# A graph layer with scatter-add: GpSimd's scatters run 16 pipeline steps behind the edges in place of 4

## The reference, cut to what matters

```python
h = max(layernorm(x), 0)
S = h[src]                                   # one row for each edge
def edge_nn(x, W, b):                        # the same weights twice
    t = relu(x @ W.T + b)
    return relu(t @ W.T + b)
msgs = edge_nn(S, W_rel[rel], b_rel[rel])
agg = segment_sum(msgs, dst, n_nodes)        # scatter-add over destinations
gates = agg @ W_ih.T + b_ih + b_hh           # i, f, g, o; f is not used
c = sigmoid(i) * tanh(g)
hn = sigmoid(o) * tanh(c)
y = relu(relu(hn @ W1.T + b1) @ W2.T + b2) @ W3.T + b3
out = x + y
```

## Time and profile before

| | us |
|---|---|
| median of 3 runs | 2260.63 (2260.33 to 2261.53) |
| the profiled execution's own time | 2269.79 |
| its span, first to last instruction | 2268.1 |
| TensorE busy | 2080.7 |
| VectorE busy | 1755.9 |
| ScalarE busy | 1627.2 |
| GpSimd busy | 1187.8 |

### The profile page before, as it was taken

One profiled execution on the slowest core, in us unless ns is written; L12 is line 12 of the kernel. 1 busy time (PEld: TensorE's weight loads), 2 busy tenths in 40 slices (PEclk: granted clock), 3 DMA queues, 4 the chain that ended last, 5 costly groups with the idle time before them and its releaser, 6 DMA issues.

```text
span 2268.1 us, 51837 instructions
## 1 busy us (share of the span) xinstructions
PE 2080.7 (92%) x14224; PEld 1405.7 (62%) x14225; DVE 1755.9 (77%) x4311; ACT 1627.2 (72%) x3364; POOL 1187.8 (52%) x917
## 2 busy tenths in 40 slices
PE   5858767767999999999999999999999999999996
PEld 4746555555666666666666666666666666445553
DVE  8537555555888888888888888888888887788886
ACT  2437655555888888888888888888888887666663
POOL 0036777777766665666666666666666644100000
PEclk7559999898999999999999999999999999999998
DMA  9954555557789898889888988888888988988886
GB/s 383 425 207 93 95 95 100 98 97 141 135 174 185 170 180 174 179 170 175 175 178 173 178 177 180 178 178 183 170 178 175 180 153 162 193 188 191 190 188 156
DMA packets 400606, 396.90 MB, mean 175 GB/s; under 512 B 263738, under 2 KB 343158, under 8 KB 394360
## 3 DMA queue, kind: packets, MB, share of 16 engines
q0 software_dynamic: 91200, 157.34, 40.8%
q1 hardware_dynamic: 306788, 238.12, 40.0%
q10 hardware_dynamic: 2516, 0.14, 0.1%
HBM read 185.88 MB, written 156.97 MB: 151 GB/s over the span
## 4 chain that ended last, share of the span: by engine, by line
PE 78%; issue 7%; POOL 5%; ACT 3%; DMA 3%; DVE 3%; another core or an unknown queue 1%; POOLq 0%; DVEq 0%; ACTq 0%; SPq 0%
PE bank L1469 33%; PE bank L1435 9%; PE bank L1416 9%; PE bank L1483 6%; PE bank L1508 5%; PE bank L1452 4%; PE bank L1398 3%; PE bank L1492 3%; POOL agg L664 2%; POOL xg L648 2%; DMA agg<-summed,scatter_idx 2%; PE bank L1308 2%; PE bank L1409 2%; PE bank L1427 1%; DMA a_lo<-row_lo 1%
## 5 line engine op out<-in xcount | busy, mean ns | idle before, releaser
L664 POOL DMA_INDIRECT agg<-summed,scatter_idx x400 | 665.5, 1664 | 501.4 <-ACT summed L724 261.4
L1469 PE MATMUL bank<-a_hi,ihT 128*128 128x512 f16 x2400 | 714.0, 379 | 2.4 <-DMA a_lo<-row_lo 2.2
L648 POOL DMA_INDIRECT xg<-in_x,src_ring x400 | 426.1, 1065 | 271.0 <-DMA src_ring<-src_slot 138.1
L1469 PE MATMUL bank<-a_lo,ihT 128*128 128x512 f16 x1200 | 454.8, 379 | 0.0
L1469 PEld LDWEIGHTS bank<-a_hi,ihT 128*128 128x128 f16 x2400 | 234.4, 98 | 213.0 <-issue 2.3
L1435 PE MATMUL bank<-relT,h_hi 128*128 x1600 | 321.5, 275 | 0.0
L1416 PE MATMUL bank<-s_hi,relT 128*128 128x256 f16 x1600 | 292.9, 278 | 0.0
L672 POOL DMA_DIRECT2D y<-in_x x100 | 133.4, 1334 | 298.0 <-DVE y L1202 287.6
L1077 DVE SCALAR_TENSOR_TENSOR h_lo<-bank,h_hi 128x512 f16<-128x512 f32 x200 | 137.5, 688 | 120.4 <-ACT h_hi L751 114.6
L757 ACT ACTIVATE xn<-xg,shift,rstd 128x256 f32<-128x256 f32 x400 | 216.4, 591 | 10.3 <-DVE shift L1111 10.3
L1070 DVE SCALAR_TENSOR_TENSOR s_lo<-bank,s_hi 128x512 f16<-128x512 f32 x200 | 136.4, 682 | 111.2 <-ACT s_hi L730 73.4
(11 more groups left out here) (197 smaller groups left out, 4642.4 us busy)
## 6 DMA issues: line engine op xcount, KB each, us to landing
agg_in<-agg SPq DMA_DIRECT2D x100, 512.0 KB
y<-in_x POOLq DMA_DIRECT2D x100, 512.0 KB
out<-y SPq DMA_DIRECT2D x100, 512.0 KB
agg<-zeros SPq DMA_DIRECT2D x24, 2112.0 KB, 15.8
dst_ring<-dst_rows SPq DMA_DIRECT2D x200, 128.0 KB
xg<-in_x,src_ring POOLq DMA_INDIRECT x400
agg<-summed,scatter_idx POOLq DMA_INDIRECT x400
src_ring<-src_slot SPq DMA_DIRECT2D x200, 1.0 KB
```

The costliest lines, as they stand in the source:

```text
L648: nc.gpsimd.indirect_dma_start(out=xg[:, k.slot(8), t, :], out_offset=None, in_=x[:, :], in_offset=bass.IndirectOffsetOnAxis(ap=src_ring[: ...
L664: nc.gpsimd.indirect_dma_start(out=agg[:, :], out_offset=bass.IndirectOffsetOnAxis(ap=scatter_idx[:, k.slot(8), t:t + 1], axis=0), in_=sum ...
L1469: last = nc.tensor.matmul(N_C[c % 2][:, 0:UNIT], lhs, rhs, start=i == 0, stop=i == len(todo) - 1)
```

## The change

The scatter of pair k moves from GpSimd's step k+4 to k+16. `summed` gets 16 slots in place of 4, `scatter_idx` 16 in place of 8. ACT's copy of the sums of pair at-4 now waits for the scatter of pair at-20, which GpSimd issues at its step at-4, as before. DVE's row numbers of pair at-3 now wait for the scatter of pair at-19, which is issued at step at-3 (before: at-7). Because a unit needs its quarter's scatters, NB goes from 54 to 66, N0 from 60 to 72 and LAST from 270 to 282. Slots must divide the unroll, so the loop bodies have 16 steps.

```diff
+SUM_SLOTS = 16
+SCATTER_LAG = 16
-NB = QUARTER_PAIRS + 4
+NB = QUARTER_PAIRS + SCATTER_LAG
 N0 = NB + 6
...
-        scatter_idx = sb("scatter_idx", [P, 8, 2], I32)
-        summed = sb("summed", [P, 4, 2, D])
+        scatter_idx = sb("scatter_idx", [P, SUM_SLOTS, 2], I32)
+        summed = sb("summed", [P, SUM_SLOTS, 2, D])
...
-        RUN = dict(loops=((16, 40), (72, 184), (216, 248)), unroll=8)
+        RUN = dict(loops=((80, 176), (224, 256)), unroll=16)
...
-                k = at - 4
+                k = at - SCATTER_LAG
...
-                            out_offset=bass.IndirectOffsetOnAxis(ap=scatter_idx[:, k.slot(8), t:t + 1], axis=0),
-                            in_=summed[:, k.slot(4), t, :], in_offset=None, compute_op=ALU.add).then_inc(scattered, 16)
+                            out_offset=bass.IndirectOffsetOnAxis(ap=scatter_idx[:, k.slot(SUM_SLOTS), t:t + 1], axis=0),
+                            in_=summed[:, k.slot(SUM_SLOTS), t, :], in_offset=None, compute_op=ALU.add).then_inc(scattered, 16)
...
-                    wait_from(act, scattered, (k.n - 3) * 32)
-                    nc.scalar.copy(summed[:, k.slot(4), :, :].rearrange("p t d -> p (t d)"),
+                    wait_from(act, scattered, (k.n - SUM_SLOTS + 1) * 32)
+                    nc.scalar.copy(summed[:, k.slot(SUM_SLOTS), :, :].rearrange("p t d -> p (t d)"),
...
-                    wait_from(dve, scattered, (k.n - 7) * 32)
-                    nc.vector.tensor_tensor(scatter_idx[:, k.slot(8), :], idx_f[:, k.slot(4), :], spare_row[:, :],
+                    wait_from(dve, scattered, (k.n - SUM_SLOTS + 1) * 32)
+                    nc.vector.tensor_tensor(scatter_idx[:, k.slot(SUM_SLOTS), :], idx_f[:, k.slot(4), :], spare_row[:, :],
                                             ALU.min).then_inc(idx_ready, 1)
```

## The result

| kernel | median us | lowest to highest | profiled execution, span |
|---|---|---|---|
| before | 2261.08 | 2260.33 to 2265.3 (4 runs) | 2269.79, 2268.1 |
| after | 2307.21 | 2300.84 to 2314.52 (4 runs) | 2300.84, 2298.8 |

The ratio is 1.0201, 95% interval 1.0168 to 1.0235: slower by 46 us, where the forecast had 17.5, and beyond the range's upper end of 2290.

The account below looks back on a forecast made before the run. PE was taken to bound the mixed and units-alone stages, the scatter cycle the later edge steps. +11.2 (edge steps) + 6.3 (DMA load at the end) = +17.5 us took the median from 2260.6 to 2278.1; range 2267 to 2290.

Parts of the forecast that it names:

- The cycle itself: Later edge steps paced by scatters: the 6.81 us scatter cycle stays, larger rings free nothing; 0, bounds 0 and 27 us.
- Twelve more edge steps: Edge-only stage: scatters start 12 early steps of 5.08 us later, less 12 x 4.15 us of PE work; +11.2 us.
- Loops: Jumps back of the 16-step bodies: nothing to gain or lose, 0; bounds 0 and 6 x 1.4 us.
- rival 3: Loop ends: jumps back to 16-step bodies stall, 6 x 2.5, some 15 us, total 2293; chance 7%.
- The stage with both: Edges and units together: scatters no longer wait for sums, PE is at 100%; 0.
- The end, DMA load: Units alone: the last 12 scatters load the DMA engines and slow transposes, 4.5 x 1.39 = 6.3 us; bounds 0 and 10.
- The end, chain: Units alone: GpSimd falls 15.6 us back at cycles of 6.93, some 20 us slack covers it; 0, upper bound 26.
- 2: Units alone: with scatter cycles of 8 us or more SP waits for scatters, +11.2 + 6.3 + 8, 2286; chance 12%.
- Rival 4: Edge stage: scatter chain freed from sums runs at GpSimd's own 6.40 us, 20 us back, 2258 or 2251; chance 9%.
- 5: Edge stage: no change in total, early edge steps at 4.15 to 4.5 us or half the chain gain, 2262; chance 6%.
- four signs: Would be wrong: scatter cadence below 6.6, early steps below 4.8, PE gaps at loop-body ends, SP waiting for scatters at L593.

Follow-up runs that it names:

- lag16_small_x: After in straight code without loops, x adds of GpSimd's steps 203 to 215 moving 16 of 128 rows: 2283.81 us, ratio 1.0119 to before.
- lag16_straight_2: After with no hardware loop, every step straight code, on one of the usual chips: 2288.78 us, ratio 1.0144 to before.
- lag16_free12: After in straight code, last 12 pairs scattered each into its own tensor, no wait between them, SP waiting for 188 pairs: 2278.5 us, ratio 1.0093 to before.
- lag16_straight_skip12: After in straight code, the last 12 pairs not scattered, SP waiting for 188 pairs: 2271.96 us, ratio 1.0065 to before.
- lag4_ring16: Before with rings of 16 sums and 16 row numbers, lag left at 4, straight code: 2262.23 us, ratio 1.0004 to before.
- lag16_again: After unchanged, run again for a second trace: 2303.42 us, ratio 1.0195 to before.
- lag4_read_first: Before with TensorE's read of the relations moved ahead of the transposes in edge steps: 2262.46 us, ratio 1.0007 to before.
- lag16_straight: After with no hardware loop, every step straight code, on the chip where before took 2269.89: 2305.08 us, ratio 1.0159 to before.
- lag16_aside: After with the last 12 pairs scattered into a second tensor, still in a chain, SP waiting for 188 pairs only: 2340.18 us, ratio 1.0307 to before.
- lag16_skip12: After, loops kept, with the last 12 pairs not scattered and SP waiting for 188 pairs: 2327.41 us, ratio 1.0249 to before.
- lag4_bodies16: Before with loop bodies of 16 steps in place of 8, lag and rings untouched: 2295.72 us, ratio 1.0112 to before.
- lag4_again: Before unchanged, run again for a trace of its own: 2262.2 us, ratio 1.0003 to before.

## Why the prediction was wrong

- *The cycle itself: 0.* Right: 6.84 us before and after; the larger rings alone change nothing.
- *Twelve more edge steps: +11.2.* Right: 8.2 and 11.7 in the two traces of after, 9.8 to 14.7 in three straight ones (`lag16_small_x`, `lag16_straight_2`, `lag16_free12`). The size of an early step was 5.08 from a trace in which it was long; in five others it is 4.8 to 4.9, and with 4.85 the forecast's own sum gives 12 x 0.70 = 8.4. The later start of the scatters was then 59.4 us (233.4 - 174.0) in place of 61.0.
- *Loops: 0.* Wrong, the first failed step. The argument from the earlier trace rows, that a dozen jumps cost 0.14 us, holds only for bodies that stay held; the prediction says so itself and then prices the case at 7%. It cost 11.5 us in one trace of after and 19.2 in the other. The 15 us of rival 3 lie between them, but by luck: the "issue" waits of the earlier trace rows that they were taken from come before 700 us, in the preparation, the edge stage and the first steps behind it, and none is at a jump between 700 and 1950.
- *The stage with both: 0.* Right but for the jumps: 9.662 to 9.669 in straight code and in bodies of 8, the one chip of the last section left out.
- *The end, DMA load: +6.3.* Right in size: in `lag16_free12` 4.4 us against its twin without these scatters, 6.2 against before. 4.8 us of its excess lie in units 66 to 71, the rest in units from 80 on, which straight code without late scatters loses as well (2.7 us in `lag16_straight_skip12`, 3.6 in `lag4_ring16`).
- *The end, chain: 0.* Wrong, the second failed step, and the term mis-sized: about 14. "So 15.6 just fits" had a slack of 20 us against a lag of 15.6 and named itself the point where it tips, at cycles of 8 us. The cycles are 8.7, and with them the prediction's own sum gives 11 x 8.68 - 60.6 - 20 = 14.9. With the 8.2 of `lag16_again` it gives 10, for the same excess of 23.3. So the sum has the right form, good to some 5 us, and the cadence in it was wrong. I had taken the last interval of the trace, one of the short kind. Its GpSimd timeline, a little earlier, has a long one that a landing ends just the same, and it was there to be read:

```profile
1897.51 1.94 POOL L664 DMA_INDIRECT agg<-summed,scatter_idx  x1 [5.94 <-ACT summed L724]
...
1906.13 2.07 POOL L664 DMA_INDIRECT agg<-summed,scatter_idx  x1 [3.88 <-DMA agg<-summed,scatter_idx]
```

That is 8.62 us, above the 8 at which the prediction says the chain binds.
- *Rivals.* 2 and 3 were priced as cases in place of each other and of the forecast. They have different causes and places, so both could come, and then 11.2 + 6.3 + 8 + 15 = 40.5 us. The range left that out. That this is so near the 40.7 of the trace is luck: the chain cost nearly twice its 8, and the other three cost less than their terms. Rival 4 (a faster scatter chain) and 5 did not come: the cadence is the landing's and GpSimd's, not the sums'.

By the parts, the first trace of after: edge stage 8.2, jumps 11.5, the end 21.3 - 0.3, of which the traffic has 4 to 6 and the chain 15 to 17; together 40.7.

Two slips of the prediction change nothing in it: it names for `g_i` and the earlier trace rows for the 0.88 us of "issue", which is the wrong way round, and the steps in straight code are 52 more, not 60.

What would show it wrong was named in the prediction, and two of four signs came: gaps of PE at the end of loop bodies, and SP waiting for scatters, at the line that is L598 here.

None of the kernels is faster than the one before; `lag4_ring16` and `lag4_read_first` equal it.

## What to carry to other kernels

When a chain of serial transfers is moved into another stage, take its cadence from that stage, with every other command in its queue counted, and not from its last interval; then follow every way back to the bound engine, since taking one wait away only showed the next. A lag and a ring that grow together free nobody: the lag costs at both ends of the pipeline, at the start as idle steps and at the end as work with no cover. A larger loop body has its own price: count the instructions of the busiest engine in a body, and look at the page's instruction queues, at the last step of each body and at the first of the next. And before the chances are set, ask of each pair of rivals whether both can come at once, since then their prices add.

## What the runs showed of the hardware beside this

On one of the chips the kernel before took 2269.89 us, on the others 2259 to 2261. The same straight code took 2305.08 there (`lag16_straight`) and 2288.78 elsewhere (`lag16_straight_2`). The traces differ in one thing that I can name: when ACT hears that PE's transposes are done, by the semaphore events. (Of the 200 such events the traces that show it lack 10 to 24, the others none.) Waits of ACT in 900:1800, first `lag16_straight`, then `lag16_straight_2`:

```profile
ACT s_hi L732 <- PE bank L1400: 77.6, 47, 2.2
ACT s_hi L732 <- remote: 42.4, 23, 2.8
```

```profile
ACT s_hi L732 <- PE bank L1400: 42.9, 46, 1.1
```

One step of `lag16_straight`, by the timelines of PE, GpSimd and ACT:

```profile
963.15 0.60 PE L1400 MATMUL bank<-ident,xn 128*128 128x128 f32 x4
...
963.99 1.65 POOL L666 DMA_INDIRECT agg<-summed,scatter_idx  x1 [0.30 <-issue]
...
965.59 0.60 ACT L732 ACTIVATE s_hi<-bank 128x512 f16<-128x512 f32 x1 [1.80 <-remote]
```

The transposes end at 963.75, but ACT starts at 965.59, about when GpSimd's issue of a scatter ends (965.64). Such semaphore events, more than 1.2 us behind the start of their transposes, number some 65 in this trace, some 90 in `lag16_aside` and in `lag16_skip12`, and 15 to 20 in the first trace of before and in `lag4_bodies16`; in all others there are none, and the event comes 0.61 us after the start. The step with both is 9.996 us in `lag16_aside` and 10.083 in `lag16_skip12` (0.05 of it step 198), where after has 9.764 and 9.832, and `lag16_skip12` is at 1.0249 where its straight twin elsewhere is at 1.0065. The late events may be the reason, but that is not shown: `lag16_straight` has some 65 of them, yet its step with both is 9.695 and its ratio 1.0159 against 1.0144 elsewhere; its loss is in the edge stage, whose step NB+20 starts 13 us later than in `lag16_straight_2`. The first trace of before has them too. It loses 10.7 us between the starts of its steps 1 and 2 (step 2 at 171.6, in `lag4_again` at 160.9), and its early steps are the prediction's 5.08. Why it differs from chip to chip, and whether GpSimd's issue holds the event or only coincides with it, stays open; no run separates them.
